# Attention and deformable convolution on one core: where the taps' hats are made, and which work stands in the front and the end

## The reference, cut to what matters

```python
x = x + attention(_gn(x))            # 8 heads of 48, 1024 tokens, softmax, projection
x = x + deform_layer(_gn(x))

# deform_layer
offset = clip(conv3x3(x, off_w) + off_b, -8, 8)          # 18 channels
mask   = 2 * sigmoid(conv3x3(x, mask_w) + mask_b)        # 9 channels
py, px = offset + pixel position + tap position          # per tap (9) and pixel
p = sum over 4 corners of x[:, y, x] * bilinear weight * mask
y = einsum('bckhw,ock->bohw', p, w) + b
yn = (y - mean) * rsqrt(var + 1e-5) * gamma + beta       # over all 8 images
return gelu(yn)
```

## Time and profile before

| | |
|---|---|
| median of 3 runs | 3497.58 us (3497.24 to 3498.59) |
| the profiled execution | 3496.99 us, span 3495.2 us |
| TensorE busy | 3234.6 us, 93% (33434 matmuls) |
| VectorE busy | 2340.7 us, 67% |
| ScalarE busy | 1670.6 us, 48% |
| GpSimd busy | 1323.7 us, 38% |
| mean granted clock of TensorE | 0.978 of full speed |
| HBM | 56.26 MB read, 34.60 MB written |

### The profile page before, as it was taken

One profiled execution on the slowest core, in us unless ns is written; L12 is line 12 of the kernel. 1 busy time (PEld: TensorE's weight loads), 2 busy tenths in 40 slices (PEclk: granted clock), 3 DMA queues, 4 the chain that ended last, 5 costly groups with the idle time before them and its releaser, 6 DMA issues. The chain is left out here.

```text
span 3495.2 us, 84765 instructions
## 1 busy us (share of the span) xinstructions
PE 3234.6 (93%) x33434; PEld 1895.0 (54%) x33434; DVE 2340.7 (67%) x3770; ACT 1670.6 (48%) x2700; POOL 1323.7 (38%) x1183
## 2 busy tenths in 40 slices
PE   5899999999999999999999999999999999998991
PEld 2265555555555555555555555555555555554660
DVE  5976677666776677866768667776677667765443
ACT  4274344644455443654437444464445544364443
POOL 0172334523354332723337233452335433263430
PEclk9799999999999999999999999999999999998995
DMA  4000000000001000000000000000000000001007
GB/s 140 19 3 37 19 1 21 2 37 19 2 21 38 1 19 2 21 38 2 20 21 3 37 19 1 21 2 37 19 2 22 38 1 1 2 21 73 1 2 325
DMA packets 12146, 97.25 MB, mean 28 GB/s; under 512 B 2813, under 2 KB 2941, under 8 KB 5008
## 3 DMA queue, kind: packets, MB, share of 16 engines
q1 hardware_dynamic: 9504, 67.40, 5.1%
q0 software_dynamic: 1152, 12.58, 0.9%
q10 hardware_dynamic: 1008, 11.01, 0.8%
HBM read 56.26 MB, written 34.60 MB: 26 GB/s over the span
## 5 line engine op out<-in xcount | busy, mean ns | idle before, releaser
L1618 PE MATMUL R<-P,WALL 128*128 128x512 f16 x3888 | 980.4, 378 | 0.3 <-issue 0.3
L636 POOL TENSOR_TENSOR PL<-P 128x1024 f16<-128x1024 f32 x256 | 617.3, 2417 | 483.7 <-ACT P L810 481.0
L1051 DVE TENSOR_REDUCE MXP<-G 128x1 f32<-128x512 f32 x926 | 631.7, 688 | 158.7 <-PE G L1375 152.0
L1597 PE MATMUL R<-MHL,XB 128*128 128x240 f16 (+14 forms) x7776 | 718.7, 234 | 2.4 <-DVE P L1291 2.4
L672 POOL TENSOR_TENSOR MHL<-M,MHL 128x280 f16<-128x280 f32 (+2 forms) x576 | 366.6, 638 | 787.5 <-ACT MHL L905 786.4
L1597 PEld LDWEIGHTS R<-MHL,XB 128*128 128x128 f16 x7776 | 580.3, 98 | 98.6 <-DVE P L1291 2.7
L810 ACT ACTIVATE P<-R 128x1024 f32<-128x1024 f32 x512 | 520.6, 1022 | 200.3 <-PE R L1420 200.1
L1618 PEld LDWEIGHTS R<-P,WALL 128*128 128x128 f16 x3888 | 377.5, 97 | 393.1 <-issue 0.5
L1123 DVE TENSOR_TENSOR PL<-P 128x1024 f16<-128x1024 f32 x256 | 487.2, 1908 | 97.2 <-ACT P L810 96.9
L1420 PE MATMUL R<-QK 48*128 48x512 f16 (+1 forms) x3072 | 422.7, 381 | 18.9 <-ACT P L810 15.6
L1268 DVE TENSOR_TENSOR M<-G,PL 128x240 f32<-128x240 f32 (+17 forms) x864 | 249.7, 319 | 271.3 <-ACT PL L895 148.3
(11 more groups left out here) (146 smaller groups left out, 3530.5 us busy)
## 6 DMA issues: line engine op xcount, KB each, us to landing
XA<-x SPq DMA_DIRECT2D x8, 1536.0 KB, 6.3
X<-x SPq DMA_DIRECT2D x8, 1536.0 KB, 6.9
x_scratch<-X SPq DMA_DIRECT2D x7, 1536.0 KB, 5.1
y_scratch<-XP ACTq DMA_DIRECT2D x7, 1536.0 KB, 5.1
WALL<-y_scratch SPq DMA_DIRECT2D x6, 1536.0 KB, 14.7
out<-WALL POOLq DMA_DIRECT2D x6, 1536.0 KB, 10.8
QK<-x_scratch SPq DMA_DIRECT2D x4, 1536.0 KB, 17.3
P<-wd SPq DMA_DIRECT2D x9, 576.0 KB, 4.9
```

The lines of the kernel that those rows point to most:

```text
L636: pool.tensor_tensor(PL[:, s % P_BUFS, :], P32[:, s % P_BUFS, :], high_view(s), ALU.subtract).then_inc(p_low_pool, 1)
L1051: dve.reduce_max(MXP[:, name[1] % 2, n // 2, n % 2:n % 2 + 1], chunk(sec, name)[:, :], AX.X).then_inc(dve_read, 1)
L1597: last = pe.matmul(out, XT[:, x_part, g * BOX_Y + r, t * 128:(t + 1) * 128], MHL[:, m_part, o + at:o + at + (hi - lo) * (x1 - x0)], start= ...
L1618: last = pe.matmul(R6[:, CT + ct, :], WALL[:, w:w + 128], PHL[:, u % 2, part // 2, t, :], start=(u % TAPS == 0 and n < CT), stop=(u % TAPS ...
```

## The change

**Hats.** `SEL`, `POSS` and the four kinds of selector matmuls go. VectorE adds the grid to the clipped offsets (`positions`), SP stores positions and masks to a DRAM scratch, and for each unit SP loads three rows, each broadcast over 128 partitions: x positions (`PX`), y positions (`PY`), mask (`PM`), one buffer each. ScalarE makes x hats for both column windows and y hats for the row windows in box layout (Abs with a per-partition bias, then Relu), GpSimd multiplies the x hats with the mask, and VectorE multiplies x and y hats, now both in SBUF. Hats are made about two units ahead. `hx`, `hy`, `pos`, `mask` are no chunks any more, so the fills stand at other places.

**Front.** START keeps the first pair's 32 maxima. The other 96 go to the attention of batch 0, 9 in 4 steps (`FIRST_FILL`), and there GpSimd makes the low half in two of three steps up to step 43.

**End.** x loads of seven images are issued by ScalarE in the last batch before its taps, y loads of two images before the last tap is done; there are areas for all eight images, except that the last y waits for the first store. The last image is stored in three pieces. Loads of the next image during the taps move from SP's queue to ScalarE's. Maxima rows are sent three units later.

```diff
 def beside(u, start):
-
-    fills = CONV_FILL[u] if start else []
-    if u + 2 >= UNITS:
-        return fills
-    return [("pos", u + 2)] + fills[:1] + [("mask", u + 2)] + fills[1:]
+    return CONV_FILL[u] if start else []
...
+def first_fills():
+
+    maxima, fills, due = MAXIMA[4 * QT:], [[] for _ in range(STEPS)], []
+    for s in range(STEPS):
+        fills[s], due = due, []
+        count = 9 * (s + 1) // 4 - 9 * s // 4
+        due = [("maxT", n[1]) for n in maxima[:count] if n[2] == 4 * QT - 1]
+        fills[s], maxima = fills[s] + maxima[:count], maxima[count:]
+    return fills
...
+POOL_STEPS = [s for s in range(STEPS) if s % 2]
+FIRST_POOL = [s for s in range(STEPS) if (s % 3 if s < 44 else s % 2)]
...
+            def positions_out(b, h):
+
+                r = h * HEAD_B
+                sp.wait_ge(pos_ready, b * 2 + h + 1)
+                sp.dma_start(pos_d[h, 0:POS_CH, :], POS[r:r + POS_CH, :]).then_inc(pos_out, 16)
+                sp.wait_ge(mask_ready, b + 1)
+                sp.dma_start(pos_d[h, POS_CH:OFF_CH, :], MSK[r + LO_ROW:r + LO_ROW + TAPS, :]).then_inc(mask_out, 16)
+
+            def spread(units_0, out_0, u):
+
+                half, tap = divmod(u, TAPS)
+
+                def row(a, n, landed):
+                    sp.dma_start(a[:, :], pos_d[half, n:n + 1, :].to_broadcast([128, HALF])).then_inc(landed, 16)
...
+                sp.wait_ge(px_used, units_0 + u)
+                row(PX, TAPS + tap, px_in)
...
+                sp.wait_ge(hats_masked, units_0 + u)
+                row(PM, POS_CH + tap, pm_in)
+                sp.wait_ge(py_used, units_0 + u)
+                row(PY, tap, py_in)
...
+                    def masked_hats(u):
+
+                        pool.wait_ge(x_hats_ready, hats_0 + (u + 1))
+                        pool.wait_ge(pm_in, landed_0 + 16 * (u + 1))
+                        for g in range(BOX_X):
+                            hat = x_hat(u, g, reach).rearrange("p (y x) -> p y x", y=HALF_ROWS)
+                            last = pool.tensor_tensor(hat, hat, window(PM[:, :], 0, HALF_ROWS, *column_window(u, g, reach)), ALU.mult)
+                        last.then_inc(hats_masked, 1)
...
+                if final:
+                    for k in range(1, BATCH):
+                        final_x(k, pieces_of(X_AT[k])[:1 if k == BATCH - 1 else None])
...
+                    def hats_x(u):
+
+                        act.wait_ge(px_in, landed_0 + 16 * (u + 1))
+                        if u >= 2:
+                            act.wait_ge(m_made, m_0 + (u - 1) * UNIT_COUNT)
+                        for g in range(BOX_X):
+                            hat = x_hat(u, g, reach).rearrange("p (y x) -> p y x", y=HALF_ROWS)
+                            last = act.activation(hat, window(PX, 0, HALF_ROWS, *column_window(u, g, reach)), ACT.Abs, bias=NEG_X[g])
+                        last.then_inc(px_used, 1)
+                        act.wait_ge(px_used, hats_0 + (u + 1))
+                        both = HXB[:, u % 2, 0:sum(x_cols(u, g, reach) for g in range(BOX_X))]
+                        act.activation(both, both, ACT.Relu, bias=1.0, scale=-1.0).then_inc(x_hats_ready, 1)
...
-                    for g in range(BOX_X):
-                        x_hats(0, g)
+                    hats_x(0)
+                    hats_y(0)
+                    if reach == NEAR_OFF:
+                        hats_x(1)
                     for c in range(ring(reach)):
                         m_halves(0, c)
...
                         for t in range(CT):
                             act.activation(PHL[:, u % 2, 0, t, :], R6[:, t, :], ACT.Copy).then_inc(p_hi, 1)
+                        if reach == NEAR_OFF and u + 2 < UNITS:
+                            hats_y(u + 2)
...
-                                last = dve.tensor_tensor(M32[:, o + at:o + at + cols], ps[:, at:at + cols],
-                                                     HX[:, u % 2, g, lo * (x1 - x0):hi * (x1 - x0)], ALU.mult)
+                            last = dve.tensor_tensor(M32[:, o + at:o + at + cols].rearrange("p (y x) -> p y x", y=hi - lo),
+                                                     window(y_hats(u, reach)[:, y:y + (hi - lo) * HW], 0, hi - lo, x0, x1),
+                                                     x_hat(u, g, reach).rearrange("p (y x) -> p y x", y=HALF_ROWS)[:, lo:hi, :],
+                                                     ALU.mult)
...
-                            if nu < UNITS and nc < BOX_X:
-                                x_hats(nu, nc)
-                            if nu < UNITS:
-                                y_hats(nu, nc)
```

More of the change, by code:

```diff
@@ L98, in ring, with x_cols, y_at, y_cols @@
     return 4 if reach == NEAR_OFF else 2
+def x_cols(u, g, reach):
+    x0, x1 = column_window(u, g, reach)
+    return HALF_ROWS * (x1 - x0)
+def y_at(u, r, reach):
+    return sum((hi - lo) * HW for n, lo, hi in row_windows(u, reach) if n < r)
+def y_cols(u, reach):
+    return y_at(u, BOX_Y, reach)
+HX_COLS = max(sum(x_cols(u, g, MAX_OFF) for g in range(BOX_X)) for u in range(UNITS))
+HY_COLS = max(y_cols(u, NEAR_OFF) for u in range(UNITS))
+if max(y_cols(u, MAX_OFF) for u in range(UNITS)) > 2 * HY_COLS:
+    raise ValueError("the far rows of one unit must fit where two near units have theirs")
 def weight(reach):
     return UNIT_COUNT // per_unit(reach)
+def hats_after(u, c, reach):
+    if reach == NEAR_OFF:
+        return u + 2 if c == 1 else UNITS
+    return u + 1 if c == per_unit(reach) - 1 - ring(reach) else UNITS
 def ahead(u, c, reach):
@@ L185, in start_chunks, with batch_chunks @@
         maxima = maxima[3:]
-    for name in maxima:
-        out.append(name)
-    for i in range(PAIRS):
-        last = out.index(MAXIMA[4 * QT * (i + 1) - 1])
-        out.insert(min(last + 5, len(out)), ("maxT", i))
-    return with_readers(out)
-def batch_chunks(start):
-    out = sum((step_chunks(s, start) for s in range(STEPS)), [])
+    return with_readers(out + [("maxT", 0)])
+def batch_chunks(start, first=False):
+    out = sum((step_chunks(s, start, first) for s in range(STEPS)), [])
     out += (DRAIN if start else []) + [("oT", CT - 1, 1)]
@@ L506, in slot, with x_hat, y_hats, window @@
             return (u * per_unit(reach) + c) % ring(reach) * size
+        def x_hat(u, g, reach):
+            at = sum(x_cols(u, n, reach) for n in range(g))
+            return HXB[:, u % 2, at:at + x_cols(u, g, reach)]
+        def y_hats(u, reach):
+            at = u % 2 * HY_COLS if reach == NEAR_OFF else 0
+            return HYB[:, at:at + y_cols(u, reach)]
+        def window(a, lo, hi, x0, x1):
+            return a.rearrange("p (y x) -> p y x", x=HW)[:, lo:hi, x0:x1]
         def in_boxes(a):
@@ L799, in after_taps, with final_x, batch @@
                 act.dma_start(y_d[bass.ds(b, 1), :, :].rearrange("a p n -> (a p) n"), YSF).then_inc(y_out, 16)
-            def batch(b, first, final):
+            def final_x(k, pieces):
+                for a, cols in pieces:
+                    act.dma_start(a, x1_d[FINAL[k], :, cols]).then_inc(xf_in[k], 16)
+            def batch(b, first, final, more):
                 sec = before_taps(b, final)
@@ L1526, in batch @@
                 last.then_inc(chunk_full, 1)
-                def hat_positions(sec, u):
-                    half = unit(u)[0]
-                    pe.wait_ge(pos_ready, b * 2 + half + 1)
-                    pe.wait_ge(mask_high_done, b * 2 + half + 1)
-                    rows = slice(0, MASK_ROW + TAPS)
-                    pe.matmul(bank(sec, ("pos", u))[:, :], SEL[rows, SELP + u % TAPS, :], POSS[rows, cols_of(half)],
-                              start=True, stop=True).then_inc(chunk_full, 1)
@@ L1538, in hat_masks @@
-                def hat_masks(sec, u):
-                    half = unit(u)[0]
-                    pe.wait_ge(mask_ready, b * 2 + half + 1)
-                    pe.matmul(bank(sec, ("mask", u))[:, :], SEL[:, SELM + u % TAPS, :], POSS[:, cols_of(half)],
-                              start=True, stop=True).then_inc(chunk_full, 1)
                 if not final:
                     next_v(0)
-                    next_v(1, 0, 3)
-                hat_positions(sec, 0)
-                if not final:
-                    next_v(1, 3)
@@ L1580, in y_hats @@
-                    def y_hats(u, c):
-                        g, x0, x1, segs, _ = made(u, reach)[c]
-                        out = bank(sec, ("hy", u, c))
-                        for n, (r, lo, hi, at) in enumerate(segs):
-                            last = pe.matmul(out[:, at:at + (hi - lo) * (x1 - x0)], SEL[:, SELY + r, :],
-                                             window(u, slice(lo, hi), x0, x1), start=(n == 0),
-                                             stop=(n == len(segs) - 1), skip_group_check=True)
-                        last.then_inc(chunk_full, weight(reach))
+                    sec = tap_sec
```

576 lines of the change are left out of this document (268 added, 308 removed).

## The result

The changed kernel takes 3374.68 us in the median of four runs (3374.22 to 3379.06), the kernel before 3497.72 on the same chip. The ratio is 0.9651, 95% interval 0.9634 to 0.9667: 123 us faster. The forecast was 3392, range 3325 to 3455.

A forecast was written before the change was run, and what follows sets the result against it. TensorE was taken to bound the attention and taps, transfers the end. Gains of 64 in seven batches' taps, 11 front, 20 end and 10 last batch sum to 105 us: 3392 from 3497.58, range 3325 to 3455.

The forecast's parts named there:

- Units with four maxima: Taps: sampling gains 1.3 us, a bank wait leaves 0.9, port contention with GpSimd leaves 0.35, in ten units a batch.
- Units 1 to 4: Taps: TensorE does not wait for the third fill; gain of 1.4 us a unit after contention.
- Units 6, 10 and 14: Taps: ScalarE reads the transposed maxima after the y hats, the third fill waits 1.8 us or more; gain 0.
- Start of a stage: Start of each taps stage: first sample 2.2 us later, unit 1 about where it was; 0, +-2 a batch.
- Last batch: Last batch's taps: 18 units gain 25 us, the start costs 15; net 10 (0 to 22).
- 6 from sharing: Last batch's start: nine x loads issued just before the first units' rows share the transfers, costing 6 us.
- Front: Attention starts some 58 us earlier, batch 0's attention takes 47 longer, set by VectorE; gain 11 (0 to 18).
- End: End after the taps: transfers set it; loads moved earlier leave 21 MB, 57 us at the same rate; gain 20.
- Rows: Broadcast rows in the taps: 2.9 us to landing, hidden by the unit's matmuls with 9 us of cover.
- A: Taps: contention and bank waits of 1.6 to 2 us in every unit leave 2 a batch; 3442 us, chance 20%.
- B: Taps: TensorE's floor is reached as VectorE catches up, bringing 17 us a batch; 3337 us, chance 18%.
- C: Taps: each of a unit's six products waits out a whole GpSimd instruction, VectorE bounds; slower, 3556 us, 6%.

The follow-up runs named there:

- the experiment: Changed kernel with the front of before (all 128 maxima in START, GpSimd in odd steps only): 3386.31 us.
- all edits: Changed kernel with later fills, transposed maxima first, y copy first, spread loads, three of four splits on GpSimd: 3225.94 us; with M before unit 1's x hats too: 3236.57.

## Why the prediction was right, and where its terms were off

The gain was 123 where I had 105, and the terms were further off than that: the full batches brought 26 more than forecast and the last batch 10 less, front and end 1 to 2 more each. Part of the closeness of the total is luck.

**Units with four maxima: right, the contention over-sized.** In batch 3 sampling was put at 4.7 and is 4.6 to 5.0; the convolution phase at 7.65 and is 7.6 to 8.3; the third fill waits for the read of the first maximum, as the later fills showed. Nine such units (5, 7 to 9, 11 to 13, 15, 16) went from 120.5 to 113.5 us in batch 3, a gain of 0.78 each. I had 0.9 and cut it to 0.35 for contention. The contention is there: in the taps of batch 3 the products went from 319 ns to 417, some 0.6 a unit, the size that I took. What was too large is its effect: I let nearly all of it delay the split and the third fill, 0.55 of 0.9, and the split starts only 0.22 later in the mean, the x hats' share included. The long products lie in the sampling of a unit, where VectorE has time for most of it. Of the two sources that I named only GpSimd's split of M does it, not the mask product. Unit 17, the tenth that I counted, gained nothing (17.39 us in both): it made no hats for a later unit before either.

**Units 1 to 4: under-sized.** 68.0 to 61.7 in all, 1.6 each instead of 1.4 (units 2 to 4 have 1.9 to 2.0, unit 1 has 0.4).

**Units 6, 10 and 14: wrong, on the hopeful side.** I gave them a gain of 0 for a third fill that waits 1.8. The wait came (5.1 us in three units), but they got slower, 40.9 to 44.0. Two things were left out. Unit 10's y copy stood behind the x hats (another 2.1 us), and after unit 14's wait TensorE ran at half clock for some ten matmuls, in six of seven full batches.

**Start of a stage: under-sized.** The chain from clip to first sample was put at 13.5 and is 12.6 (1499.15 to 1511.74). The first sample came 1.3 later, but unit 0 went from 14.1 to 10.5, without the hats, a V chunk and the stops for them. That is 2.3 a batch where I had 0. Per batch the four terms give 7.0 + 6.3 - 3.0 + 2.3 = 12.6, against 9.1, and 12.8 is what the 89.8 come to.

**Last batch: the step that failed most.** I took 15 for the start and 25 for the units. The units gave 18.5 (206.8 to 188.3, with the units from 2 on at 9.5 to 10.0 each, save unit 10's 11.3), the start cost 16.8, and with an attention 1.7 longer nothing is left. The step that failed is "6 from sharing": spreading the loads gave 20 back, 15 of it before the first sample. With them spread the start is 51.0 against 49.2 before, so the 4 from the chain and the 5 at half clock were too much, and the sharing, with the clock that falls in the longer idle time (0.75, then 0.83), was nearly all. The units then give 22.9 (206.8 to 183.9), near the 25.

**Front: right in size, its reason only in part.** 12.3 (or 11.6 by the experiment) against 11. The first exponential came at 99.9 for 101 to 103. (96 maxima left the front, not the 92 of the text; the sum has 2.25 x 43 and is right.) But "VectorE over 90% busy" is wrong: it is at 110 of 144. TensorE's granted clock was 0.93 in that window, and a step is as long as I worked out without any engine being full. Moving four splits off VectorE still gave 4.6 us. How the rest divides between bank waits and clock stays open.

**End: right.** 21.7 against 20; 378 GB/s against 367.

**Rows: right for full batches.** 3.2 us against 2.9, and between units 2 and 17 of batch 3 no idle time released by them. The lower end of the line, at 36 KB, is 1.5 and not 1.4; nothing hangs on it. The test with doubled rows shows that the last batch had some 5 us of cover at most, not the 9 that I claimed for all.

**The rivals.** A (bank waits eat the gain) had the wait right, but 0.97 in the mean of batch 3's nine (8.7 in all) rather than 1.6 to 2. B (TensorE's floor) had too high a floor: it gave the taps 17 a batch, and with all edits middle part and taps of batch 3 take 285.1 instead of 315.4, 30 less. It took the removed matmuls for 19.6 us a batch, and TensorE's busy time in the taps of batch 3 fell by 25.4, of which a V chunk that moved ahead of the stage is 1.6. C (whole GpSimd instructions) happens in a fifth of the products, where I had it in all, and delays the split by at most 0.2 us a unit.

## What to carry to other kernels

Taking chunks out of a queue that alternates between two banks moves all that is behind them forward: look again at where the remaining ones stand. Moving the third and the fourth by three or four matmuls was worth 82 us here, two thirds of what the whole change had brought. When work moves to an engine that has time, check what it is queued ahead of there; two reads of PSUM behind hats cost 46 and 12. Bulk loads issued ahead of a chain of small transfers cost the chain, not themselves; issue them once it is under way. And before a gain of a few microseconds is put down to an edit, look in several batches whether slow matmuls only fell elsewhere.

## What the runs showed of the hardware

Of 864 products on VectorE with both inputs in SBUF, 322 overlapped a GpSimd split. 164 of these started after the split, ended only after it, and took 0.45 to 0.91 us where the median product takes 0.36. With one input in PSUM 443 overlapped one, and the longest of all was 0.41. The Trainium skill (SBUF — State Buffer, "SBUF: two separate sides") has this as an exclusive lock held for a whole instruction, and the trace agrees for these 164. The splits agree with it too: where a product had started first, they took 0.72 us in the median, alone 0.64.

After idle times of only 2 us TensorE's clock sometimes fell: 0.72 in the 6.2 us behind the one of unit 14, 1.00 in the 12 us before, and so in six of seven full batches. Behind the 2.09 us of unit 10 and the 1.75 of unit 14 in batch 0 the matmuls kept their 0.216 us.

A row of 2 KB, broadcast over 128 partitions from DRAM, landed in 3.2 us in the median of 288 and in 10.6 beside loads of 10.5 MB on another queue. It is read once for each partition: reads of HBM rose from 56.26 to 168.72 MB, by 112.5, where 432 rows of 0.262 MB are 113.2, and the kernel with 408 more rows read another 106.96, which is 408 times 0.262.
